# Attention kernel: causal masks applied on the Vector engine, query and key copies on the Scalar engine, one transposed bank ahead of each pair of scores

## The reference

```python
q = (x @ wq).reshape(b, s, 32, 16).transpose(0, 2, 1, 3)
k = (x @ wk).reshape(b, s, 8, 16).transpose(0, 2, 1, 3)
v = (x @ wv).reshape(b, s, 8, 16).transpose(0, 2, 1, 3)
q, k = _apply_rope(q, cos, sin), _apply_rope(k, cos, sin)
k, v = jnp.repeat(k, 4, axis=1), jnp.repeat(v, 4, axis=1)
scores = jnp.einsum('bhqd,bhkd->bhqk', q, k) / HEAD_DIM ** 0.5
scores = jnp.where(causal[None, None], scores, -jnp.inf)
probs = jax.nn.softmax(scores, axis=-1)
out = jnp.einsum('bhqk,bhkd->bhqd', probs, v)
```

## Time and profile before

| | |
|---|---|
| median of 3 runs | 2930.53 (2928.91 to 2933.16) |
| the profiled execution | 2930.81 |
| its span, first to last instruction | 2929.1 |
| PE busy in the span | 2793.4 (95%) |
| DVE busy | 1236.7 (42%) |
| ACT busy | 877.9 (30%) |
| POOL busy | 838.8 (29%) |
| mean granted clock of TensorE | 0.982 |

### The profile page before, as it was taken

The page is one execution under the profiler, slowest core; times in us unless marked ns, Lnnn a source line. Parts: engine busy times, 40 slices in busy tenths (PEclk is TensorE's granted clock), DMA queues, the critical chain, the costliest instruction groups (busy, mean ns, idle before and its releaser), DMA issues.

```text
span 2929.1 us, 45881 instructions
## 1 busy us (share of the span) xinstructions
PE 2793.4 (95%) x16150; PEld 2283.9 (78%) x16150; DVE 1236.7 (42%) x2152; ACT 877.9 (30%) x1697; POOL 838.8 (29%) x1306
## 2 busy tenths in 40 slices
PE   6989999988999939999999999999999999999998
PEld 6865555556666529999999999999999999999997
DVE  6756777747888833332232232132133133133111
ACT  1126666641555512221121121122122122122110
POOL 4546776631166641101101111011021021011010
PEclk9999999999999969999999999999999999999999
DMA  3101222242122223221122032032033033022010
GB/s 109 43 1 31 48 45 48 55 92 87 68 84 75 77 83 106 91 86 64 51 92 75 26 108 83 15 109 87 12 108 101 11 100 104 14 90 85 26 47 21
DMA packets 97078, 194.68 MB, mean 66 GB/s; under 512 B 22126, under 2 KB 23758, under 8 KB 96800
## 3 DMA queue, kind: packets, MB, share of 16 engines
q1 hardware_dynamic: 75072, 131.77, 15.1%
q0 software_dynamic: 21856, 60.73, 6.6%
HBM read 148.77 MB, written 38.94 MB: 64 GB/s over the span
## 4 chain that ended last, share of the span: by engine, by line
PE 62%; DMA 0%; POOL 0%; DVE 0%; issue 0%; ACT 0%; DVEq 0%; POOLq 0%
PE ex_hid L1775 31%; PE ex_acc L102 10%; PE ex_acc L103 10%; PE ex_acc L104 10%; PE ex_xb L1745 1%; DMA ex_ys<-xn_dram,ex_slot_gather 0%; POOL out_dram L1627 0%; POOL ex_ys L1607 0%; DVE ex_ys L1688 0%; POOL ex_xg L1592 0%; DMA ex_ys<-slot_table_dram 0%; PE ex_acc L1745 0%; DVE ex_h0l L1696 0%; ACT ex_h0h L1655 0%; DVE ex_xT0l L1671 0%
## 5 line engine op out<-in xcount | busy, mean ns | idle before, releaser
L1696 DVE SCALAR_TENSOR_TENSOR ex_h0l<-ex_hid,ex_h0h 128x640 fp32r<-128x640 f32 x128 | 105.5, 824 | 682.8 <-ACT ex_h0h L1655 682.8
L1696 DVE SCALAR_TENSOR_TENSOR ex_h1l<-ex_hid,ex_h1h 128x640 fp32r<-128x640 f32 x128 | 105.4, 824 | 602.9 <-ACT ex_h1h L1655 602.3
L1655 ACT ACTIVATE ex_h0h<-ex_hid 128x640 fp32r<-128x640 f32 x128 | 90.1, 704 | 734.5 <-PE ex_hid L1775 734.5
L1655 ACT ACTIVATE ex_h1h<-ex_hid 128x640 fp32r<-128x640 f32 x128 | 90.1, 704 | 729.8 <-PE ex_hid L1775 729.8
L654 DVE TENSOR_REDUCE at_nb<-at_ring 128x2 f32<-128x512 f32 (+1 forms) x384 | 246.8, 685 | 121.1 <-PE at_ring L760 120.9
L1597 POOL COPY ex_gi<-ex_slot_gather 128x1 int32 (+1 forms) x82 | 15.3, 187 | 918.2 <-PE ex_xb L1745 913.3
L102 PE MATMUL ex_acc<-ex_w_h,ex_h1h 128*128 128x512 f32 x640 | 254.8, 398 | 0.0
L102 PE MATMUL ex_acc<-ex_w_h,ex_h0h 128*128 128x512 f32 x640 | 253.4, 396 | 0.0
L103 PE MATMUL ex_acc<-ex_w_l,ex_h0h 128*128 128x512 f32 x640 | 250.3, 391 | 0.0
L103 PE MATMUL ex_acc<-ex_w_l,ex_h1h 128*128 128x512 f32 x640 | 250.2, 391 | 0.0
L104 PE MATMUL ex_acc<-ex_w_h,ex_h1l 128*128 128x512 f32 x640 | 249.8, 390 | 0.0
(11 more groups left out here) (273 smaller groups left out, 5665.2 us busy)
## 6 DMA issues: line engine op xcount, KB each, us to landing
ex_raw<-in_w_tiles_dram SPq DMA_DIRECT2D x256, 256.0 KB, 2.8
x_in<-in_x_dram SPq DMA_DIRECT2D x32, 256.0 KB, 2.7
act<-at_raw SPq DMA_DIRECT2D x128, 64.0 KB
at_recb<-o_rec_dram SPq DMA_DIRECT2D x16, 512.0 KB
k<-in_x_dram SPq DMA_DIRECT2D x32, 256.0 KB, 2.7
cx_ctx<-in_ctx_dram SPq DMA_DIRECT2D x16, 512.0 KB, 3.8
out_dram<-cx_res SPq DMA_DIRECT2D x16, 512.0 KB, 2.8
xn_dram<-cx_prob SPq DMA_DIRECT2D x16, 512.0 KB, 2.8
```

What stands on the lines that cost most here:

```text
L1655: act.activation(h[f % 2][0][:], hid[:, :, 0:HB], ACT.Relu).then_inc(sm["h_hi"], 1)
L1696: dve.scalar_tensor_tensor(h[f % 2][1][:], hid[:, :, 0:HB], 0.0, f32(h[f % 2][0][:]), ALU.max, ALU.subtract).then_inc(sm["h_lo"], 1)
```

## The change

PE no longer adds the mask. DVE does, head by head, with an instruction that adds the mask to the scores in PSUM, negates the sum, takes its minimum over the keys (the negated maximum) and writes the sum back in place; the mask tile is widened to 256 columns, the first 128 of them zero. DVE's copies of qc and k go to ACT. There is now one turn in front of each pair of scores: k at p = 0, m at p = 1, qa to qd at p = 2 to 5, and `TURNS` is changed to that order. On ACT the copies of the queries stand ahead of the exponentials of p = 2 to 5; the copy of k stands behind those of p = 0, that of the maxima behind those of p = 1. The hunks that are left out widen the tile, add the constant LARGEST (3e38), drop the semaphore `q_dve`, and adapt the lines ahead of the first half.

```diff
@@ -414,7 +415,7 @@
         block = s.ctx.enter_context(nc.Block())
         BLOCKS = ((0, 0), (0, 1), (1, 1))
 
-        TURNS = ("s0", "s1", "m", "qa", "s2", "s3", "s4", "s5", "qb", "qc", "s6", "s7", "s8", "s9", "qd", "k", "s10", "s11")
+        TURNS = ("k", "s0", "s1", "m", "s2", "s3", "qa", "s4", "s5", "qb", "s6", "s7", "qc", "s8", "s9", "qd", "s10", "s11")
         QUERIES = {"qa": (0, 0), "qb": (0, 2), "qc": (1, 0), "qd": (1, 2)}
 
         def bank(e, name):
...
@@ -563,11 +564,15 @@
 
         @block.scalar
         def _(act):
-            def keep_q(h, i, name, x, n):
+            def keep_q(h, i, name, x):
                 act.wait_ge(sm["q_turned"], ONE + 4 * h + 1 + sorted(QUERIES).index(name))
                 gh, c = QUERIES[name]
                 act.activation(qs[i][:, gh, c:c + 2, :].rearrange("p h n -> p (h n)"), x[:], ACT.Copy,
                                scale=HD ** -0.5).then_inc(sm["q_act"], 1)
+
+            def keep_k(h, i, x):
+                act.wait_ge(sm["k_turned"], ONE + h + 1)
+                act.activation(ks[i][:].rearrange("p g n -> p (g n)"), x[:], ACT.Copy).then_inc(sm["k_kept"], 1)
 
             def keep_sums(h, qb, i, b):
                 act.wait_ge(sm["sums"], ONE + 3 * h + (1 if qb == 0 else 3))
...
@@ -576,12 +581,16 @@
                 act.activation(raw[i][:, qb, :], pv[:], ACT.Copy).then_inc(sm["sums_kept"], 1)
 
             def first():
-                for n, name in enumerate(("qa", "qb", "qd")):
-                    keep_q(0, 0, name, bank(1, name), n)
+                for name in ("qa", "qb", "qc", "qd"):
+                    keep_q(0, 0, name, bank(1, name))
+                keep_k(0, 0, bank(1, "k"))
 
             def step(j, w, q, e):
                 h = 2 * j + e
                 for p in range(6):
+                    if p >= 2 and within(h + 1, 0, HALVES):
+                        name = sorted(QUERIES)[p - 2]
+                        keep_q(h + 1, (2 * q + e + 1) % 4, name, bank(e, name))
                     if within(h - 2, 0, HALVES):
                         for r in range(2):
                             n = 2 * p + r
...
@@ -590,7 +599,9 @@
                             if r == 0 and p % 2 == 0:
                                 wait(act, sm["sums"], 3 * (h - 2) + p // 2 - 1)
                             act.activation(pT[slot][:], st[n % 3][:], ACT.Exp).then_inc(sm["probs"], 1)
-                    if p == 0 and within(h - 1, 0, HALVES):
+                    if p == 0 and within(h + 1, 0, HALVES):
+                        keep_k(h + 1, (2 * q + e + 1) % 4, bank(e, "k"))
+                    if p == 1 and within(h - 1, 0, HALVES):
                         act.wait_ge(sm["m_turned"], ONE + h)
                         act.activation(mT[(e - 1) % 2][:], bank(e, "m")[0:32, 0:P], ACT.Copy).then_inc(sm["m_kept"], 1)
                     if p == 2 and within(h - 3, 0, HALVES):
...
@@ -624,24 +632,12 @@
 
         @block.vector
         def _(dve):
-            def keep_q(h, i, x):
-                dve.wait_ge(sm["q_turned"], ONE + 4 * h + 3)
-                gh, c = QUERIES["qc"]
-                dve.tensor_scalar(qs[i][:, gh, c:c + 2, :].rearrange("p h n -> p (h n)"), x[:], HD ** -0.5, None,
-                                  ALU.mult).then_inc(sm["q_dve"], 1)
-
-            def keep_k(h, i, x):
-                dve.wait_ge(sm["k_turned"], ONE + h + 1)
-                dve.tensor_copy(ks[i][:].rearrange("p g n -> p (g n)"), x[:]).then_inc(sm["k_kept"], 1)
-
             def first():
                 for x in qst:
                     dve.memset(f32(x[:, :, :, :, 48:64]), 0.0).then_inc(sm["filled"], 1)
                 dve.memset(f32(kst[:, :, :, 48:64]), 1.0).then_inc(sm["filled"], 1)
                 for x in vc:
                     dve.memset(x[:], 1.0).then_inc(sm["filled"], 1)
-                keep_q(0, 0, bank(1, "qc"))
-                keep_k(0, 0, bank(1, "k"))
 
             def step(j, w, q, e):
                 h = 2 * j + e
...
@@ -649,15 +645,15 @@
                     if within(h, 0, HALVES):
                         for r in range(2):
                             n = 2 * p + r
-                            heads, qb = (slice(0, REP), 0) if p < 2 else (slice(p // 2 * 2 - 2, p // 2 * 2), 1)
-                            dve.wait_ge(sm["scores"], ONE + PIECES * h + n + 1)
-                            dve.tensor_reduce(nb[e][:, r, p % 2, heads, qb],
-                                              bank(e, f"s{n}")[:].rearrange("p (h k) -> p h k", h=heads.stop - heads.start),
-                                              AX.X, ALU.max, negate=True).then_inc(sm["maxima"], 1)
-                    if p == 2 and within(h + 1, 0, HALVES):
-                        keep_q(h + 1, (2 * q + e + 1) % 4, bank(e, "qc"))
-                    if p == 4 and within(h + 1, 0, HALVES):
-                        keep_k(h + 1, (2 * q + e + 1) % 4, bank(e, "k"))
+                            x = bank(e, f"s{n}")
+                            wait_apart(dve, sm["scores"], PIECES * h + n + 1, passed_dve)
+                            width, qb, heads = (P, 0, range(REP)) if p < 2 else (S, 1, range(p // 2 * 2 - 2, p // 2 * 2))
+                            for c, a in enumerate(heads):
+                                y = x[:, c * width:c * width + width]
+                                m = dve.tensor_tensor_reduce(y, y,
+                                                             t["mask"][:, S - width:S], -1.0, LARGEST, ALU.add, ALU.min,
+                                                             nb[e][:, r, p % 2, a, qb:qb + 1])
+                            m.then_inc(sm["maxima"], 1)
                     if e == 1 and p == 5 and within(j - 2, 0, B):
                         dve.wait_ge(sm["den_loaded"], ONE + 16 * (j - 2) + 16)
                         wait_apart(dve, sm["rec_stored"], 16 * (j - 2), passed_dve)
...
@@ -711,10 +707,8 @@
                     pe.wait_ge(sm["m_kept"], ONE + h)
                 if last == "k" and within(h + 1, 0, HALVES):
                     pe.wait_ge(sm["k_kept"], ONE + h + 2)
-                if last == "qc" and within(h + 1, 0, HALVES):
-                    pe.wait_ge(sm["q_dve"], ONE + h + 2)
-                if last in ("qa", "qb", "qd") and within(h + 1, 0, HALVES):
-                    pe.wait_ge(sm["q_act"], ONE + 3 * h + 4 + ("qa", "qb", "qd").index(last))
+                if last in QUERIES and within(h + 1, 0, HALVES):
+                    pe.wait_ge(sm["q_act"], ONE + 4 * h + 5 + sorted(QUERIES).index(last))
                 return bank(e, name)
 
             def turn_q(h, e, name):
...
@@ -754,12 +748,10 @@
                 for c, n in enumerate(heads):
                     for r in range(2):
                         rows = slice(64 * r, 64 * r + 48)
-                        pe.matmul(banks[r][:, c, :], qs[i][rows, p % 2, n, width - P:width],
-                                  ks[i][rows, p % 2, 0:width], start=True, stop=False, skip_group_check=True)
-                for r in range(2):
-                    pe.matmul(banks[r][:, :, width - P:width], t["identb"][:],
-                              t["mask"][:].unsqueeze(1).to_broadcast([P, len(heads), P]), start=False, stop=True,
-                              skip_group_check=True).then_inc(sm["scores"], 1)
+                        m = pe.matmul(banks[r][:, c, :], qs[i][rows, p % 2, n, width - P:width],
+                                      ks[i][rows, p % 2, 0:width], start=True, stop=True, skip_group_check=True)
+                        if c == len(heads) - 1:
+                            m.then_inc(sm["scores"], 1)
 
             def shifted(h, i, p):
                 kb, qb = BLOCKS[p // 2]
...
@@ -798,23 +789,21 @@
                 live_s, live_d = within(h, 0, HALVES), within(h - 2, 0, HALVES)
                 i_s, i_d = (2 * q + e) % 4, (2 * q + e - 2) % 4
                 if live_s:
-                    pe.wait_ge(sm["q_act"], ONE + 3 * h + 3)
-                    pe.wait_ge(sm["q_dve"], ONE + h + 1)
+                    pe.wait_ge(sm["q_act"], ONE + 4 * h + 4)
                     pe.wait_ge(sm["k_kept"], ONE + h + 1)
                 if live_d:
                     pe.wait_ge(m_loaded[i_d], ONE + 32 * (w - 1 + q) + 32)
                 for p in range(6):
                     if live_d:
                         shifted(h - 2, i_d, p)
+                    if p == 0 and within(h + 1, 0, HALVES):
+                        turn_k(h, j, e)
+                    if p == 1 and within(h - 1, 0, HALVES):
+                        turn_m(h, e)
+                    if p >= 2 and within(h + 1, 0, HALVES):
+                        turn_q(h, e, sorted(QUERIES)[p - 2])
                     if live_s:
                         score(j, q, e, p)
-                    if p == 0 and within(h - 1, 0, HALVES):
-                        turn_m(h, e)
-                    if within(h + 1, 0, HALVES):
-                        for name in {0: ("qa",), 2: ("qb", "qc"), 4: ("qd",)}.get(p, ()):
```

(16 more changed lines are left out.)

## The result

The changed kernel takes 3036.74 us (median of 4 runs, 3015.91 to 3052.18) against 2931.85 before: 1.0352 times as long, 95% interval 1.0289 to 1.0416. That is slower, as forecast, but by 105 us where 40 were forecast, and outside the range. The profiled execution took 3038.78, its span is 3037.0 and its mean granted clock .946. The slowest run has the lowest mean clock (.943 at 3052.18) and the fastest the highest (.956 at 3015.91).

The account below looks back on a forecast made before the run. The prediction took PE, busy 59.06 of 60.00 us, as the bound. A half of 4.74 + 2 x 4.79 = 14.32, 1.41 over 12.91, in 29 steps gave +41: 2930.5 + 41 = 2971, range 2945 to 3012.

Parts of the forecast that it names:

- Masks off TensorE: On PE, removing the mask matmuls saves 1.8 us a half, 58 us over 32 halves, were PE to stay full.
- Pairs 2 to 5: Each two pairs last 4.79 against 4.08 and 4.10 before, as PE waits .82 for ACT's exponential.
- Pairs 0 and 1: Together they last 4.74 against 4.73 before, the masks' gain of .88 going to DVE.
- DVE's first piece: At p = 0 DVE's first piece takes 1.28 and PE follows .06 later, with scores of p = 1 at 3.16.
- The result's instruction: DVE's instruction writing a head's result costs .09, the lower bound; upper bounds were .17 and .20.
- The .10 for DVE's own wait: At p = 0, .10 more before DVE starts, an estimate, its wait now being an instruction of its own.
- +1.41: The whole half of the attention stretch grows by 1.41, from 12.91 to 14.32.
- the .87 (3.16 - 2.29): Ahead of the scores of p = 1, DVE lets PE go at 3.16; PE alone would be there at 2.29.
- a granted clock under 1.00 in the stretch: Sign of being wrong: the clock falls in the attention stretch now that PE rests; not in the sum.
- DVE becomes the bound: Rival: DVE's result instructions hide nothing, half 15.4 with waits, 3003, or 3044 without any overlap; chance .12.
- DVE alone holds PE: Rival: DVE, not ACT's chain, holds PE; half 13.05, +4, 2935; chance .07.
- PE's own work sets the half: Rival: PE waits for neither ACT nor DVE; half 11.81, -32, 2899; chance .08.

Follow-up runs that it names:

- experiment 9: Kernel before with only the mask matmuls taken out, maxima over all keys by plain reductions, order and copies as before: 2874.77 us, ratio 0.9812.
- experiment 11: Changed kernel's order of turns and ACT's copies, but no mask for the maxima on any engine and plain reductions on DVE: 2946.95 us, ratio 1.0055.
- experiment 1: Changed kernel with TensorE's rests filled by spare transposes at p = 1, 3 and 5: 2986.88 us, ratio 1.0228.
- experiment 5: Changed kernel with DVE's steps written out one after another instead of looped: 3008.84 us, ratio 1.0264.
- experiment 6: Changed kernel with TensorE's rests filled by extra transposes and DVE's steps written out instead of looped: 2972.54 us, ratio 1.0152.
- experiment 10: Kernel before without mask matmuls, maxima over all keys, plus three TensorE rests a half ahead of the values: 3025.20 us, ratio 1.0305.
- experiment 7: Kernel before, masks kept on TensorE, with only rests added for TensorE ahead of the values at p = 1, 3 and 5: 3010.21 us, ratio 1.0278.
- experiment 3: Changed kernel with ACT's copies of the queries behind the exponentials of the same p instead of ahead: 3016.72 us, ratio 1.0275.
- experiment 8: Kernel before with only the 256 wide masks (p = 2 to 5) on DVE, order and copies as before: 2940.70 us, ratio 1.0037.

## Why the prediction was wrong

- **The terms at the full clock came out near.** Masks off TensorE: 1.8 a half forecast, 12.90 - 10.97 = 1.93 measured (before, and experiment 9). Pairs 2 to 5: 4.79 for two, 4.69 measured. Pairs 0 and 1: 4.74, 4.61 measured; DVE's first piece holds PE for 1.15 there (601.60 to 602.75) where 1.34 was put, because a head and its result take .25 or .38 from start to start (601.82 to 602.07, 606.40 to 606.78) where .30 and .43 were put. The result's instruction hides behind the next head, so its lower bound was the right choice, and DVE did not become the bound. The .10 for DVE's own wait had no row behind it; from the scores to DVE's start it takes .85 (600.75 to 601.60), and .70 with the plain wait of experiment 11 (403.32 to 404.02). From run to run: 12.90 - 1.93 + 2.49 (the order, 13.46 - 10.97) + .54 (DVE's masks, 14.00 - 13.46) = 14.00, +1.10 a half where +1.41 was forecast.
- **One agreement is luck.** By the forecast's steps the order without DVE's wait is 1.65 + 2.22 + 2 x 4.79 = 13.45, and experiment 11 measured 13.46. But its pairs 0 and 1 last 4.04 (402.31 to 406.35), not 3.87, since PE waits for the plain reductions there, and its other pairs 4.71, not 4.79. So the .54 above is what DVE's masks add to that wait, and not the whole of the .87 (3.16 - 2.29) forecast.
- **The step that failed** is the one that left the clock out: "a granted clock under 1.00 in the stretch, now that PE rests, which would add to all of this and is not in the sum". The text took the 1.00 of the earlier trace rows along into a kernel whose mix on TensorE it changed; it named the fall as a sign of being wrong, but gave it no price and no chance, so neither the range nor a rival holds it. In its place experiments 1, 5 and 6 show 64 us by the falls of the clock and DVE's late starts, more than the forecast's whole loss. The late starts by themselves are the small part, by estimate 4 x 1.7 = 7, from the halves of 15.87 and 15.89 that experiment 1 has at 1.00 beside its 14.14. In the profiled execution the halves whose mean clock is under 1.00 last 69 longer than 14.0 each, and 31 of that lie in the first five (213.96 to 315.46, mean clock .57), which follow the low clock at the start of the stage.
- **A term that was missing:** DVE's late start in the first half of a round, some 2 us. The text counted DVE's 64 instructions by their time alone, and not by what they are in a loop. With the rests filled, DVE's loop is worth 2986.88 - 2972.54 = 14 us; in the changed kernel roughly 28, as some falls of the clock begin there (the half at 419.11).
- **The rivals.** That DVE becomes the bound, that DVE alone holds PE, and that PE's own work sets the half were all rightly held unlikely: DVE is busy for 11.05 of a half of 14.01, PE waits for both ACT and DVE. None of them has the clock in it.
- **Which way** was right, and why: the new order, with ACT's copies ahead of the exponentials, and DVE's latency at p = 1 cost more than the masks.

The Trainium skill, "TensorE: Matmul & The Clock Gate", A second HAM failure mode: psum-queue depth-cycling, describes a kernel whose TensorE idles briefly and often between groups of matmuls, goes back and forth between the two clock levels, and loses by it. The changed kernel (.84 over the 24 halves from 254.32 on) and experiment 10 agree with it; experiment 7, with more rest and a clock of 1.00, shows that brief rests alone do not decide it.

What stays open: which property of the matmuls holds the clock up, and which rests it takes without them. Mask matmuls held it up, and so did spare transposes in the rests (experiments 1 and 6). Busy shares do not put the kernels in order: without masks, experiment 3 rests no more than the changed kernel and falls more (.74 against .84).

## What to carry to other kernels

Work taken off TensorE can have a price where TensorE also begins to wait: look at both together, give a fall of the granted clock a price and a chance in the forecast, and give the new version a run with the rests filled, which parts the cost of the waits from that of the clock. A copy put ahead of the work that another engine waits for is paid by that engine: without masks the new order of turns and copies costs 2.49 us a half (experiments 9 and 11), and with the copies back behind the exponentials the changed kernel's half goes from 14.0 to 12.9 to 13.2 at the full clock (experiment 3). The cheapest way to spare work is to leave it out: the maxima need no mask, since they only shift the exponent and the mask is applied later; without it the kernel takes 2874.77, 1.9% less than before, and is the best version found. That this stays exact for other inputs is argued and not tried: it needs scores whose unmasked maximum is not far above the masked one.

## What was not expected of the hardware

The low clock can hold while TensorE is busy. In experiment 3, over a half:

```profile
408.87:429.14 20.27, 19.78 (x94) 9.65 (x90) 11.26 (x66) 10.22 (x20) 8.62 (x14) 0.50 0.21 45
```

PE is busy 19.78 of 20.27 at .50, and the clock does not rise in it. The groups by line and form of the changed kernel show an instruction over one head and one for its result, whose lengths (456, 325 and 140 ns) add up to more than they take in a row:

```profile
L653 DVE CUSTOM_DVE_ANT_0 at_ring<-at_ring,mask 128x256 f32<-128x256 f32 x512 | 201.9, 456 | 122.4 <-PE at_ring L751 122.2
...
L653 DVE DVE_READ_ACCUMULATOR2_ANT at_nb<- 128x1 f32 x1024 | 143.0, 140 | 0.1
...
L653 DVE CUSTOM_DVE_ANT_0 at_ring<-at_ring,mask 128x128 f32<-128x128 f32 x512 | 130.2, 325 | 50.3 <-PE at_ring L751 41.0 <-issue 8.6
```

And DVE came 2.31 late at the start of a round of its loop, which it did not do with its steps written out, nor with the 12 reductions a half of the kernel before, nor in experiment 8, where DVE has some 41 instructions a half in place of 65 to 68.
